# A PSUM bank changes rings in the feed-forward stage of a six-stage decoder kernel

## The reference

```python
x = _layernorm(x + _L0_attn_ref(x, ...))        # stage A: causal attention, 16 heads
x = _layernorm(x + _L0_xattn_ref(x, ctx, ...))  # stage B: cross attention to 64 tokens
x = _layernorm(x + _L0_ffn_ref(x, ...))         # stage C: linear plus gated LoRA
x = _layernorm(x + _L1_attn_ref(x, ...))        # stage D: flow attention
x = _layernorm(x + _L1_xattn_ref(x, ctx, ctx))  # stage E: cross attention
x = _layernorm(x + _L1_ffn_ref(x, ...))         # stage F: below
```

```python
h = bit_linear(x, w1)            # 512 -> 2048; x rounded to 8 bits a row, w1 ternary
h = depthwise_conv1d(h, conv_w, conv_b)   # three taps along the tokens
h = silu(h)
return bit_linear(h, w2)         # 2048 -> 512; h rounded to 8 bits a row, w2 ternary
```

## Time and profile before

| | |
|---|---|
| device time, median of 3 runs | 2610.78 us (2606.73 to 2611.08) |
| device time of the profiled execution | 2607.08 us |
| its span, first to last instruction | 2605.3 us |
| TensorE busy | 2349.7 us (90%) |
| VectorE busy | 1588.0 us (61%) |
| ScalarE busy | 1243.8 us (48%) |
| GpSimd busy | 690.0 us (26%) |
| mean granted TensorE clock | 0.982 of full speed |

### The profile page before, as it was taken

How to read it: one execution, slowest core, us unless ns; L and a number is a source line. 1 busy time by engine, 2 the same in 40 slices (tenths; PEclk the granted TensorE clock), 3 DMA queues, 4 the chain that set the end, 5 groups by cost and what they waited for, 6 DMA issues and landing times.

```text
span 2605.3 us, 37008 instructions
## 1 busy us (share of the span) xinstructions
PE 2349.7 (90%) x12984; PEld 1304.5 (50%) x13000; DVE 1588.0 (61%) x3101; ACT 1243.8 (48%) x2870; POOL 690.0 (26%) x989
## 2 busy tenths in 40 slices
PE   7989999889988999998898999988899899999866
PEld 3655544445565544444556554444455655444343
DVE  4664633569866462447977655165797746516588
ACT  5763212259775422127967441222886723122396
POOL 0002231027401232013820213101480031400266
PEclk9999999999999999999999999999999999999889
DMA  8001100010210200001030110101003010100000
GB/s 300 18 11 49 39 29 33 1 49 1 89 49 10 72 29 17 32 1 49 9 128 2 54 28 29 32 17 42 8 9 128 2 58 23 45 1 1 0 1 33
DMA packets 58987, 99.41 MB, mean 38 GB/s; under 512 B 13364, under 2 KB 13748, under 8 KB 58296
## 3 DMA queue, kind: packets, MB, share of 16 engines
q1 hardware_dynamic: 58808, 97.06, 11.1%
HBM read 88.66 MB, written 8.39 MB: 37 GB/s over the span
## 4 chain that ended last, share of the span: by engine, by line
PE 62%; ACT 17%; DVE 16%; issue 4%; POOL 0%; DMA 0%; ACTq 0%; DVEq 0%; POOLq 0%; SPq 0%
PE psum L398 21%; PE psum L392 13%; ACT prob L810 7%; PE psum L424 4%; PE psum L483 3%; DVE neg_max L1109 3%; PE psum L549 2%; DVE f_a L1116 2%; PE psum L791 2%; ACT xT L846 2%; DVE f_top L1396 1%; ACT f_z L1011 1%; ACT f_a L1009 1%; PE psum L569 1%; DVE f_g L1386 1%
## 5 line engine op out<-in xcount | busy, mean ns | idle before, releaser
L392 PE MATMUL psum<-xT,weights 128*128 128x512 f32 x768 | 335.0, 593 | 6.0 <-ACT xT L846 6.0
L398 PE MATMUL psum<-weights,mixed 128*128 128x512 f32 x768 | 339.1, 597 | 0.0
L810 ACT ACTIVATE prob<-psum,neg_max 128x128 f32<-128x128 f32 (+3 forms) x512 | 265.0, 544 | 109.6 <-DVE neg_max L1109 109.6
L1434 POOL TENSOR_SCALAR var<-stats 128x1 f32<-128x1 f32 x192 | 61.2, 319 | 788.3 <-DVE stats L1060 788.3
L1109 DVE TENSOR_REDUCE neg_max<-psum 128x1 f32<-128x128 f32 (+3 forms) x512 | 217.5, 483 | 81.3 <-PE psum L488 46.6
L1447 POOL TENSOR_TENSOR f_a<-f_a,f_z 128x256 f32<-128x256 f32 x256 | 205.2, 812 | 114.1 <-DVE f_a L1116 110.8
L398 PEld LDWEIGHTS psum<-weights,mixed 128*128 128x128 f32 x768 | 144.6, 192 | 179.9 <-issue 179.2
L392 PEld LDWEIGHTS psum<-xT,weights 128*128 128x128 f32 x768 | 144.0, 190 | 180.1 <-issue 172.2
L398 PE MATMUL psum<-weights,xT 128*128 128x512 f32 x512 | 231.4, 596 | 2.4 <-DVE recip L1299 1.6
L1090 DVE TENSOR_TENSOR x<-psum,x 128x512 f32<-128x512 f32 x128 | 88.4, 691 | 225.4 <-PE psum L398 163.5
L846 ACT COPY xT<-psum 128x512 f32<-128x512 f32 x128 | 67.1, 596 | 327.7 <-PE psum L451 327.7
(11 more groups left out here) (246 smaller groups left out, 4271.8 us busy)
## 6 DMA issues: line engine op xcount, KB each, us to landing
xT<-in_xT SPq DMA_DIRECT2D x8, 1024.0 KB, 6.2
x<-in_x SPq DMA_DIRECT2D x8, 1024.0 KB, 8.9
out<-x SPq DMA_DIRECT2D x16, 512.0 KB, 2.8
weights<-in_a_k SPq DMA_DIRECT2D x4, 1024.0 KB, 5.2
weights<-in_a_q SPq DMA_DIRECT2D x4, 1024.0 KB, 5.0
weights<-in_a_v SPq DMA_DIRECT2D x4, 1024.0 KB, 5.1
w1f<-in_w SPq DMA_DIRECT2D x4, 1024.0 KB, 15.0
w2f<-in_w SPq DMA_DIRECT2D x4, 1024.0 KB, 17.3
```

Of the source, the lines that this page charges most:

```text
L392: last = mm(bank[:, 0:n], weights[weight][:, c, heads(g)], rhs(c), start=(c == 0), stop=(c == C - 1))
L398: last = mm(bank, lhsT(c), weights[weight][:, c, :], start=(c == 0), stop=(stop and c == C - 1))
L810: last = run(sb["prob"][:, slot, o:o + keys], bank[:, o:o + keys], ACT.Exp, bias=sb["neg_max"][:, n, qc, j:j + 1], accum_out=sb["a_sum"][: ...
```

## The change

A ring gets a method `give`. At step (0, 12) of stage F, in every batch, TensorE first waits until ScalarE has freed everything that it holds in its ring. Then the ring's last bank, bank 2, is taken from it and put in front of the banks of VectorE's ring, whose other three follow from the oldest on. From there VectorE's ring has four banks and ScalarE's two. At `a_end` of the next batch the shares are set back to three and three.

```diff
+WIDEN = (0, 12)
...
+    def give(self, pe, ring):
+
+        self.drained(pe)
+        bank = self.banks.pop()
+        n = len(ring.names) - ring.first
+        k = n % len(ring.banks)
+        ring.banks = [bank] + ring.banks[k:] + ring.banks[:k]
+        ring.first = len(ring.names)
...
                 elif kind == "a_end":
                     for ring in (a_ring, turn_ring, turn_act_ring):
                         ring.drained(pe)
+                    act_ring.banks, dve_ring.banks = banks[0:3], banks[3:6]
...
                     if m == 0 and s < W:
                         taken(pe, ("f_unit", s))
                         pe.wait_ge(q["f_pad"], at("f_pad", 4))
+                    if (s, m) == WIDEN:
+                        act_ring.give(pe, dve_ring)
                     bank = dve_ring.claim(pe, step)
```

## The result

| | before | changed |
|---|---|---|
| median of 4 runs each | 2608.76 us (2606.13 to 2611.08) | 2623.49 us (2622.25 to 2625.98) |
| ratio, 95% interval | | 1.006 [1.0047, 1.0072] |
| span of the profiled execution | 2605.3 us | 2624.2 us |
| TensorE busy | 2349.7 us | 2368.9 us |
| VectorE, ScalarE, GpSimd busy | 1588.0, 1243.8, 690.0 us | 1586.6, 1244.1, 690.0 us |

The forecast was +3.9 us and the range ended at 2621. It became 14.7 us by the medians and 18.9 by the two profiled spans; the profiled one of before lies low among its runs and that of the changed kernel high among its own. The other engines did the same work in the same time. TensorE is busy 19 us more with the same instructions, so the clock has to be looked at before any wait.

A forecast was written before the change was run, and what follows sets the result against it. VectorE, with ScalarE nearly as full, was taken to set the pace, not TensorE. Batches 0 to 2 gave 3 x (1.9 + 0.6 - 1.4) = +3.3 us, batch 3 +0.6: +3.9, so 2614.7 us, range 2606 to 2621.

The forecast's parts named there:

- The new wait: At tile 12, batches 0 to 2: TensorE stands still 2.8 us for ScalarE's ring, 1.9 us of it remaining.
- The swallowing: Behind tile 13: VectorE's waits for ScalarE of 0.20, 0.55 and 0.20 us absorb 0.95 of the 2.8 us delay.
- The clock after the new wait: Behind tile 12: a clock fall adds 0.6 us a batch in batches 0 to 2, nothing in batch 3.
- The fourth bank: After 606 us in stage F: VectorE's waits for TensorE shrink, gaining 1.4 us a batch, bounds 0 and 2.9.
- The reading of VectorE's 2.9 us as its ceiling: After 606 us: VectorE waits for TensorE seven times, 2.9 us in all, the upper bound of the bank's gain.
- The longer taps: While GpSimd is full: a shared SBUF port turns VectorE's savings into longer taps, sum up to 3 us higher.
- Two banks for ScalarE: ScalarE's ring in stage F: claims wait for the bank two back, cost 0, up to 0.5 us a batch if late.
- The reading of the tightest claim: The projection at 610.89 was taken as ScalarE's tightest claim, with 0.97 us of room.
- Batch 3: Stage F of batch 3: 1.0 us lost at tile 12, 0.4 us gained from the bank, +0.6 us together.
- The end of the batch: From f_part to the last norm: the rings don't touch what this goes through, so 0.
- Elsewhere: From a_end to step 12: the waits are those of before and resetting the shares costs no instruction.
- slower by more: Rival: clock falls behind tile 12 every time (+1.4), bank returns only 0.7; +8.8 us, 2619.6 us; chance 0.37.

The follow-up runs named there:

- wait_only: Changed kernel with the wait at tile 12 kept but no bank handed over, both rings staying at three; 2618.33 us, ratio 1.004.
- after_covered: Changed kernel with filler matmuls in the idles at tile 12, f_part(2,0,2), d_sums, d_sums2 and b_rows(0,0); 2604.78 us, ratio 0.9984.
- oldest_covered: Changed kernel handing over ScalarE's longest-claimed bank without the ring-emptying wait, fillers at f_part(2,0,2), d_sums, d_sums2 and b_rows(0,0); 2602.07 us, ratio 0.9976.
- two_banks: Kernel before, but ScalarE's ring gives up its longest-claimed bank at step (0, 12) and nobody gets it; 2606.2 us, ratio 0.9992.
- oldest_bank: Changed kernel handing over ScalarE's longest-claimed bank, waiting only for that bank's own copy instead of the whole ring; 2613.11 us, ratio 1.002.
- give_later: Changed kernel with the hand-over at step (1, 4) instead of (0, 12), still waiting for ScalarE's empty ring; 2613.6 us, ratio 1.0018.
- before_shift: Kernel before with 5 extra matmuls at the start of stage D in every batch; 2618.46 us, ratio 1.0039.
- after_filled_d: Changed kernel with filler matmuls at d_sums, d_sums2 and b_rows(1,0), the last misplaced outside the idle; 2618.28 us, ratio 1.0036.
- fill_wait: Changed kernel with 12 filler matmuls ahead of the wait at tile 12 in batches 0 to 2; 2625.0 us, ratio 1.0066.
- before_covered_e: Kernel before with fillers at b_rows(0,0), d_sums, d_sums2 and ahead of stage E's third and fourth transposes of x; 2596.44 us, ratio 0.9962.

## Why the prediction was wrong

**The new wait** (1.9 us a batch, bounds 1.0 to 2.8). The 2.8 us of standstill are exact. What is left of it without the clock and the bank is wait_only less the fall: 3.3 - 1.7 = 1.6 us at the end of F, and after_covered against oldest_covered gives 1.6 as well. Right within 0.3. The swallowing was right too: of the 4.4 us at tile 13, 3.5 are left at the f_top before the scale, 0.9 less, where 0.95 was forecast.

**The clock after the new wait** (0.6 us). Mis-sized: 1.7 us, in each of the three batches. It fell every time, and nothing of the fall passed beside the work that counts. The bound of 1.7 was right; taking 1.2 of it for overlap and half of that for chance was not. A standstill right before the work that VectorE waits for puts the fall on that very work.

**The fourth bank** (1.4 us, bounds 0 to 2.9). Mis-sized: 0.5 us. The reading of VectorE's 2.9 us as its ceiling was right, and so was "hardly passed on". What I took for gone, TensorE's ring waits, moved to f_scale, where it waits 3.2 us for f_diag. VectorE's waits went to 1.8 us, not near 0. The longer taps of the earlier trace rows do not explain what is missing: from tile 12 to the last tile of batch 0 the taps take 35.9 us in two_banks, 36.4 in oldest_bank and 35.4 in give_later, and the last two end alike.

**Two banks for ScalarE** (0). Right in its size, by two_banks. The reading of the tightest claim was not: it was put at the earlier trace rows with 0.97 us of room, and two_banks waits 0.8 us at the half projection behind tile 12. In the changed kernel the new wait hides that one.

**Batch 3** (1.0 and -0.4). Nearly nothing in all, +0.04, for other reasons: wait_only costs 2.8 us there and the bank gives 2.8 of it back. Without the wait it gives 0.9. The clock is part of it: between 60 and 105 us of this stage F its mean is 0.89 in wait_only and 0.96 in the changed kernel. VectorE's waits for TensorE, from which the 0.4 was taken, are 0.9 us there and not 0.7: the earlier trace rows leaves out one of 0.2 for f_g.

**The end of the batch** (0). Failed. By its banks and waits the sentence was true, but the idle ahead of f_part grew from 1.11 to 2.06 us and the clock fell there in two of three batches, 1.5 us each. The fourth bank is behind it: wait_only and two_banks keep the 1.1 us, oldest_bank has 2.06. In the traces with the 2.06 us open the clock fell there in 8 of 18 batches, in those with the 1.1 us in none of 18; with the idle filled, in six kernels and 18 batches, never.

**Elsewhere** (0). This is the step that failed most: 7.4 us in the profile shown, of which 1.8 came with the execution, and 5.5 in the second. "From a_end to step 12 the waits are those of before" is true and not enough. The waits are the same, and their consequences are not: idles at d_sums and d_sums2 that passed unnoticed in before are followed by half clock when the batch lies elsewhere in time. before_shift brings such falls about with no change of banks, and after_filled_d and after_covered take them away with the change in place.

**The sum.** Stage F: 3 x (1.6 + 1.7 - 0.5) + 2 x 1.5 = 11.4 us, measured 11.5. Outside 5.5 to 7.4. Together 16.9 to 18.8, where the two profiles are 17.1 and 18.9 us longer than that of before. The rival "slower by more" had the mechanism in F (2.6 us a batch against 2.8 measured), and I gave it too little; its sum too stopped at the edge of stage F.

**What stays open.** That a batch's place sets the falls was shown by moving it, not worked out ahead: 1.0 us is enough, but no run tested a shift that was forecast to be harmless. In batch 3 the clock goes with the bank's 2.8 us behind the late start, but what would be left without it was not tested. And what the change is worth when both kernels have the same fillers was not measured for the change as it stands.

## What to carry to other kernels

Before costing a wait on TensorE, list the idles of the whole trace that are followed by full clock although like ones are followed by half clock: they are a debt that a shift of a microsecond can call in, be it a delay of 1.0 us in another stage (before_shift) or a gain of 0.5 us (oldest_bank, which turned into a loss). Cover such idles with matmuls into the bank that the waiting step is about to overwrite, and look in the trace that the filler lies in the wait: one that doesn't costs its length. And when a shared buffer is handed over, hand over the one that its owner has held longest: the new owner gets as much, and here 0.8 us of waiting behind tile 12 stood in the place of 2.8 ahead of it. Compare a change with a kernel before that has the same fillers, or the fillers are credited to the change.

## What the runs showed that I had not expected

- A fall costs by its place. Behind tile 12 it costs 1.7 us of 1.7 possible, the pair in stage D 2.6 us (501.7 against 499.1).
- In one comparison, 30 runs of the kernel before lie between 2605.39 and 2611.14 us. The second profile of the changed kernel shows one source of such a spread: the same program, the same stage F, and 1.9 us less in batch 0, where it had no falls in stage D.
- Filler matmuls of 0.21 us hold the clock through a wait of 2.8 us (fill_wait) without delaying what waits. With them in four kinds of idle, and no change of banks, the kernel before is 0.4% faster (before_covered_e), 11.6 us against the 2.3 that the bank gives in stage F (two_banks to oldest_bank, 0.5 three times and 0.9).
